# Sliding attention, 32 clips: heads taken in alternating order, the value products one clip later, and the output's bias copy on ACT between the exponentials

## What is computed

```
h  = token block(x)                 # top-k attention, feed-forward 512, convolution of 3, max over pairs: 32 x 125 x 128
n  = (h - mean) / sqrt(var + eps)   # over the features
q, k, v = n @ W_qkv + b_qkv
p  = softmax over the keys at most 32 steps away of (q . k) / 4
h  = h + (p @ v) @ W_proj + b_proj
out = h + (h - mean) / sqrt(var + eps)
```

## Time and profile before

| | |
|---|---|
| median of three runs | 547.76 us |
| the profiled execution, its own time | 550.68 us |
| its span, first to last instruction | 548.9 us |
| mean granted TensorE clock, share of full | 0.947 |
| PE / DVE / ACT / POOL busy, whole span | 92% / 74% / 65% / 60% |
| first scores of the sliding attention | 389.45 us |
| last instruction on POOL (output of clip 31) starts | 545.74 us |

### The profile page before, as it was taken

One profiled execution on the slowest core, in us unless ns is written; L12 is line 12 of the kernel. 1 busy time (PEld: TensorE's weight loads), 2 busy tenths in 40 slices (PEclk: granted clock), 3 DMA queues, 4 the chain that ended last, 5 costly groups with the idle time before them and its releaser, 6 DMA issues.

```text
span 548.9 us, 13987 instructions
## 1 busy us (share of the span) xinstructions
PE 503.3 (92%) x4554; PEld 355.3 (65%) x4554; DVE 408.9 (74%) x1728; ACT 358.4 (65%) x1072; POOL 329.2 (60%) x367
## 2 busy tenths in 40 slices
PE   6998899999998599999999999997599999999983
PEld 4778666666665357766667776655367766776762
DVE  3797757888886367787877777865369988898993
ACT  5985558889887244454455445453578888888881
POOL 2860647778886556776666676663126555565654
PEclk9999559999999699999999999999779999999997
DMA  4440212222222010000000000000000000000000
GB/s 163 138 161 11 64 34 51 56 62 62 63 60 75 20 37 20 19 20 22 35 22 20 19 20 20 1 1 1 0 2 2 20 21 20 13 11 21 20 21 20
DMA packets 21946, 19.89 MB, mean 36 GB/s; under 512 B 14210, under 2 KB 18466, under 8 KB 21746
## 3 DMA queue, kind: packets, MB, share of 16 engines
q1 hardware_dynamic: 21298, 18.28, 11.6%
q10 hardware_dynamic: 576, 0.71, 0.4%
HBM read 16.81 MB, written 2.18 MB: 35 GB/s over the span
## 4 chain that ended last, share of the span: by engine, by line
PE 44%; DVE 15%; issue 4%; ACT 2%; POOL 2%; POOLq 0%; DVEq 0%; ACTq 0%
PE quad L802 10%; PE quad L779 9%; PE bank L824 6%; PE bank L888 4%; PE bank L899 4%; DVE quad L1156 4%; PE bank L905 3%; PE quad L771 2%; PE bank L880 2%; DVE z_all L1186 2%; DVE otok L1168 2%; DVE st_all L1188 2%; DVE wmax L1156 2%; PE bank L793 1%; PE bank L817 1%
## 5 line engine op out<-in xcount | busy, mean ns | idle before, releaser
L476 POOL TENSOR_SCALAR put<-keyb,c 100x1000 f32<-100x1000 bf16 x32 | 89.0, 2782 | 47.9 <-DMA keyb<-key_scratch 26.3
L972 ACT ACTIVATE wprobs<-quad,wmax 125x125 f32<-125x125 f32 x256 | 75.5, 372 | 19.7 <-DVE wmax L1156 19.7
L1156 DVE CUSTOM_DVE_ANT_0 quad<-quad,c 125x125 f32<-125x125 f32 x256 | 66.1, 311 | 9.1 <-PE quad L847 9.1
L609 ACT ACTIVATE probs<-quad,negmax 100x250 f32<-100x250 f32 x128 | 58.3, 467 | 21.8 <-DVE negmax L561 20.9
L779 PE MATMUL quad<-h1T,w 128*128 128x500 f32 x128 | 61.9, 609 | 0.7 <-ACT hid L943 0.6
L802 PE MATMUL quad<-w,hid 128*125 128x128 f32 x512 | 58.8, 273 | 0.1
L802 PEld LDWEIGHTS quad<-w,hid 128*125 128x125 f32 x512 | 57.3, 188 | 0.8 <-issue 0.5
L1058 POOL TENSOR_TENSOR kbd<-wkT,c 128x250 f32<-128x250 f32 x32 | 19.2, 600 | 53.0 <-ACT wkT L980 53.0
L491 PE MATMUL bank<-c,probs 100*125 100x100 f32 x256 | 48.3, 316 | 2.2 <-ACT probs L609 1.4
L491 PEld LDWEIGHTS bank<-c,probs 100*125 100x125 f32 x256 | 36.8, 209 | 20.6 <-issue 13.2
L943 ACT ACTIVATE hid<-quad,vec_cols 128x500 f32<-128x500 f32 x64 | 43.0, 675 | 7.4 <-PE quad L779 4.1
(11 more groups left out here) (131 smaller groups left out, 1267.9 us busy)
## 6 DMA issues: line engine op xcount, KB each, us to landing
keyb<-key_scratch SPq DMA_DIRECT2D x64, 97.7 KB
xa<-xT SPq DMA_DIRECT2D x8, 500.0 KB, 3.6
xt<-xtok SPq DMA_DIRECT2D x16, 250.0 KB
out<-o_all SPq DMA_DIRECT2D x7, 250.0 KB
w<-weights SPq DMA_DIRECT2D x1, 1024.0 KB, 7.2
vec_rows<-rows SPq DMA_DIRECT2D x1, 448.0 KB, 5.2
c<-consts ACTq DMA_DIRECT2D x1, 428.5 KB, 6.5
w<-weights ACTq DMA_DIRECT2D x1, 192.0 KB, 4.2
```

What stands on the lines that cost most here:

```text
L476: nc.gpsimd.tensor_scalar(put[u % 3][:, :, :], keyb[p][:, :, :], c[0:ROWS, CONST["sidx"]], None, ALU.is_equal).then_inc(put_done, 1)
L609: nc.scalar.activation(probs[p][:, ch, :], s_bank[ch][0:ROWS, 0:L], ACT.Exp, bias=negmax[p][:, ch:ch + 1], accum_out=rowsum[p][:, ch:ch + ...
L972: ins = nc.scalar.activation(probs[p][:, j, :], s_of(j), ACT.Exp, bias=negmax[p][:, j:j + 1], scale=-1.0)
L1156: ins = nc.vector.tensor_tensor_reduce(s_of(j), s_of(j), c[0:LH, CONST["band"]], 1.0, OFF, ALU.add, ALU.min, negmax[p][:, j:j + 1])
```

## The change

- The order of the heads is a table, ORDER = (0, 2, 4, 6, 1, 3, 5, 7), so that two successive heads lie in different PSUM banks. Each mask and each exponential has its own semaphore count and its own wait; masks 4 to 7 of the order wait for the exponential 0 to 3 that reads the same bank.
- The value products of a clip are issued one window later (u-2), and in PE's queue between the k/q products and the v product. They no longer wait for oF, but for otok of the clip before and oT. vo has three buffers.
- All that follows them (oT, y_a, otok, oF, projection, z, statistics, output) is one window later too, so there is one more window at the end (u = 34 on PE, ACT and DVE, 35 on POOL, each one more than before).
- PE issues the transposes of oT ahead of the transposes of the probabilities. ACT issues oT between kT and qT.
- oF moves from DVE to ACT, behind the exponential number 5 of the order and ahead of numbers 6 and 7.
- On DVE z stands ahead of the copy probsT, the statistics behind it. otok is written in the heads' own order through a permuted access pattern.
- y_of and y_proj lie in columns 256 and 384 of y_bank.

```diff
-        vo = pair("vo_", [LH, H, CW])
+        vo = [sb(f"vo_{i}", [LH, H, CW]) for i in range(3)]
-        y_a, y_of, y_proj = y_bank[0:LH, 256:512], y_bank[:, 0:LH], y_bank[0:LH, 256:256 + D]
+        y_a, y_of, y_proj = y_bank[0:LH, 256:512], y_bank[:, 256:256 + LH], y_bank[0:LH, 384:384 + D]
+        ORDER = (0, 2, 4, 6, 1, 3, 5, 7)
...
@@ PE
+                if within(u, 3, B + 3):
+                    pe.wait_ge(oT_done, u - 2)
+                    for i in range(2):
+                        ins = nc.tensor.transpose(y_a[:, 128 * i:128 * i + 128], oT[:, LH * i:LH * i + LH], ident)
+                    ins.then_inc(otok_ready, 1)
+
                 if within(u, 1, B + 1):
-                    pe.wait_ge(exp_done, 4 * u)
+                    pe.wait_ge(exp_done, H * u)
...
+                if within(u, 2, B + 2):
+                    wait(pe, otok_done, u - 2)
+                    wait(pe, oT_done, u - 2)
+                    pe.wait_ge(pT0_done, u - 1)
+                    pe.wait_ge(pT1_done, u - 1)
+                    pe.wait_ge(v_done, u - 1)
+                    if u == 2:
+                        pe.wait_ge(n3T_done, NP)
+                    for j in range(H):
+                        ins = nc.tensor.matmul(y_bank[CW * (j % 4):CW * (j % 4) + CW, LH * (j // 4):LH * (j // 4) + LH],
+                                               vo[(u - 2) % 3][:, ORDER[j], :], probsT[p][:, j, :], start=True, stop=True)
+                    ins.then_inc(pv_ready, 1)
+
...
-                if within(u, 1, B + 1):
-                    wait(pe, oF_done, u - 1)
-                    pe.wait_ge(pT0_done, u)
-                    pe.wait_ge(pT1_done, u)
-                    pe.wait_ge(v_done, u)
...
-                if within(u, 2, B + 2):
-                    pe.wait_ge(oF_done, u - 1)
+                if within(u, 3, B + 3):
+                    pe.wait_ge(oF_done, u - 2)
                     nc.tensor.matmul(y_proj, oF[:, :], w[:, WEIGHT["wp"]], start=True, stop=True).then_inc(proj_ready, 1)
...
@@ ACT
+                def exponents(lo, hi):
+
+                    for k in range(lo, hi):
+                        j = ORDER[k]
+                        act.wait_ge(min_done, H * u + k + 1)
+                        nc.scalar.activation(probs[p][:, j, :], s_of(j), ACT.Exp, bias=negmax[p][:, j:j + 1], scale=-1.0).then_inc(exp_done, 1)
...
+                if within(u, 3, B + 3):
+                    act.wait_ge(pv_ready, u - 2)
+                    wait(act, otok_ready, u - 3)
+                    wait(act, z_done, u - 3)
+                    nc.scalar.activation(oT[:, :], y_bank[:, 0:2 * LH], ACT.Copy).then_inc(oT_done, 1)
+                if within(u, -1, B - 1):
                     wait(act, scores, u)
                     nc.scalar.activation(qT[pn][:, :], x_q, ACT.Identity, bias=col("wq_b")).then_inc(qT_done, 1)
...
                 if within(u, 0, B):
                     wait(act, pT0_ready, u - 1)
-                    exponents(0)
-                    exponents(1)
+                    exponents(0, 2)
                 if within(u, 1, B + 1):
                     act.wait_ge(pT1_ready, u)
                     wait(act, pv_ready, u - 2)
                     nc.scalar.activation(probsT[1 - p][:, 4:8, :].rearrange("p h l -> p (h l)"), t_bank[1][0:LH, 0:4 * LH], ACT.Copy).then_inc(pT1_done, 1)
                 if within(u, 0, B):
-                    exponents(2)
-                    exponents(3)
+                    exponents(2, 6)
+                if within(u, 3, B + 3):
+                    act.wait_ge(oF_ready, u - 2)
+                    wait(act, proj_ready, u - 3)
+                    nc.scalar.activation(oF[:, :], y_of, ACT.Identity, bias=col("wv_b")).then_inc(oF_done, 1)
+                if within(u, 0, B):
+                    exponents(6, 8)
...
@@ DVE
+                b = u - 3
+                def mask_and_min(lo, hi):
+
+                    for k in range(lo, hi):
+                        j = ORDER[k]
+                        if k >= 4:
+                            dve.wait_ge(exp_done, H * u + k - 3)
+                        nc.vector.tensor_tensor_reduce(s_of(j), s_of(j), c[0:LH, CONST["band"]], 1.0, OFF, ALU.add, ALU.min,
+                                                       negmax[p][:, j:j + 1]).then_inc(min_done, 1)
+                if within(u, 0, B):
+                    dve.wait_ge(scores, u + 1)
+                    mask_and_min(0, 2)
+                if within(u, 3, B + 3):
+                    dve.wait_ge(otok_ready, b + 1)
                     nc.vector.reciprocal(rinv[:, :], y_a.rearrange("p (h f) -> p h f", h=H)[:, :, HD]).then_inc(rinv_done, 1)
+                    dve.wait_ge(rinv_done, b + 1)
+                    wait(dve, oF_ready, b)
+                    nc.vector.tensor_tensor(otok[:, :].rearrange("p (k c f) -> p c k f", k=4, c=2),
...
+                if within(u, 0, B):
+                    mask_and_min(2, 6)
+                if within(u, 0, B):
+                    mask_and_min(6, 8)
+                if within(u, 3, B + 3):
+                    dve.wait_ge(proj_ready, b + 1)
...
+                    nc.vector.tensor_tensor(z_all[:, b:b + 1, :], y_proj.unsqueeze(1), z_all[:, b:b + 1, :], ALU.add).then_inc(z_done, 1)
+                if within(u, 0, B):
                     dve.wait_ge(pT0_ready, u + 1)
                     wait(dve, pv_ready, u - 1)
                     nc.vector.tensor_copy(probsT[p][:, 0:4, :].rearrange("p h l -> p (h l)"), t_bank[0][0:LH, 0:4 * LH]).then_inc(pT0_done, 1)
...
+                if within(u, 3, B + 3):
+                    dve.wait_ge(z_done, b + 1)
+                    nc.vector.bn_stats(zst[:, b, :], z_all[:, b, :]).then_inc(stat, 1)
+                    dve.wait_ge(stat, b + 1)
+                    nc.vector.bn_aggr(mvz[:, b, :], zst[:, b, :]).then_inc(mean_done, 1)
```

More of the change, by code:

```diff
@@ L827, in ffn @@
                     ins.then_inc(conv_ready, 1)
-            pe.wait_ge(ones_in, 2)
+            pe.wait_ge(ones_in, 3)
             def window(h, p):
@@ L844, in window @@
                     pe.wait_ge(kbd_done, u + 1)
-                    wait(pe, exp_done, 4 * u)
+                    wait(pe, exp_done, H * u)
                     for cc in range(4):
@@ L966, in window @@
                 _, _, pn = shift(h, p, 1)
-                def exponents(cc):
-                    act.wait_ge(min_done, 4 * u + cc + 1)
-                    for j in range(2 * cc, 2 * cc + 2):
-                        ins = nc.scalar.activation(probs[p][:, j, :], s_of(j), ACT.Exp, bias=negmax[p][:, j:j + 1], scale=-1.0)
-                    ins.then_inc(exp_done, 1)
+                def exponents(lo, hi):
[3 more added lines that the diff above has]
+                        nc.scalar.activation(probs[p][:, j, :], s_of(j), ACT.Exp, bias=negmax[p][:, j:j + 1], scale=-1.0).then_inc(exp_done, 1)
                 if within(u, -1, B - 1):
@@ L984, in window @@
                     act.wait_ge(v_ready, u + 1)
-                    wait(act, pv_ready, u - 1)
-                    nc.scalar.activation(vo[p][:, :, 0:HD], x_v.rearrange("p (h f) -> p h f", h=H), ACT.Copy).then_inc(v_done, 1)
-                if within(u, 2, B + 2):
-                    act.wait_ge(pv_ready, u - 1)
-                    wait(act, otok_ready, u - 2)
-                    wait(act, z_done, u - 2)
-                    nc.scalar.activation(oT[:, :], y_bank[:, 0:2 * LH], ACT.Copy).then_inc(oT_done, 1)
+                    wait(act, pv_ready, u - 2)
+                    nc.scalar.activation(vo[u % 3][:, :, 0:HD], x_v.rearrange("p (h f) -> p h f", h=H), ACT.Copy).then_inc(v_done, 1)
                 if within(u, 0, B):
                     wait(act, pT0_ready, u - 1)
-                    exponents(0)
-                    exponents(1)
+                    exponents(0, 2)
                 if within(u, 1, B + 1):
@@ L1000, in window @@
                 if within(u, 0, B):
-                    exponents(2)
-                    exponents(3)
+                    exponents(2, 6)
[5 more added lines that the diff above has]
+                    exponents(6, 8)
             in_turn(act, ffn, window)
-            at(window, B)
-            at(window, B + 1)
+            for u in range(B, B + 3):
+                at(window, u)
         @block.gpsimd
@@ L1073, in _ @@
             in_turn(pool, ffn, window)
-            for u in range(B, B + 3):
+            for u in range(B, B + 4):
                 at(window, u)
@@ L1142, in ffn @@
                     stats(1, t2, 4, t + 1)
-            for i in range(2):
+            for i in range(3):
                 nc.vector.memset(vo[i][:, :, HD:CW], 1.0).then_inc(ones_in, 1)
@@ L1148, in window @@
                 u, _, _ = shift(h, p, 0)
-                um2, _, _ = shift(h, p, -2)
-                def mask_and_max(cc):
-                    if cc == 0:
-                        dve.wait_ge(scores, u + 1)
-                    for j in range(2 * cc, 2 * cc + 2):
```

(24 more changed lines are left out.)

44 lines of the change are left out of this document (14 added, 30 removed).

## The result

The kernel after takes 557.08 us (median of four runs, 556.37 to 557.75), the kernel before beside it 547.62 (four runs, 546.08 to 548.02): ratio 1.0178 [1.0153, 1.0203]. It is slower by 9.5 us; the forecast was 555.7, slower by 7.9. The profiled execution took 556.59 us, its span is 554.7. The ratios here leave out executions more than 1.5% above the fastest of their kernel.

What follows compares the result with a forecast made beforehand. Bound taken as a DVE, PE, DVE loop of 4.367 us. New period 4.58: 28 x 0.213 = 6.0, minus 1.5 at the head, plus 3.4 at the tail, +7.9 us, so 555.7 us; range 550.5 to 562.5.

Steps and rivals of the forecast that it cites:

- So +3.4: Tail of the sliding attention: one more window after the last scores was to add 3.4 us.
- The clock rival: Sliding attention: PE idles in each window, its clock drops, and each ten windows cost 25 us; chance 0.03.
- The head: First windows of the sliding attention: 0.9 and 0.6 us saved, 1.5 together.
- The 0.6 forecast for the next window: Window 2 has no z yet, so window 3's first mask follows after 3.84 in place of 4.45 us.
- A second path ties with it.: Kernel before: mask, four exponentials, then probability transposes were said to tie with the DVE, PE, DVE loop at the period, 4.37.
- 0.24 saved at the first exponential: ACT's first exponential waits for one mask instead of two and starts 0.43 us after the first mask.
- 0.57 off the path.: PE's queue: value products moved between the k/q and v products, a clip later, were to leave the chain, saving 0.57 us.
- PE alone, at most 4.2: PE's own work per window, from its 9.66 busy of 10 us, was put at no more than 4.2 us.
- the loop of 4.15 through oT: Loop z, oT, its transposes, otok, value products, back to z, with v product and a hop: 4.15 us.
- Faster: Alternating heads shorten mask and exponential pitches; period towards 4.10, total 542.2 us; chance 0.07.
- No change: Pitches shrink half way, or ACT's order matters less: period 4.26 to 4.34, total within 0.2%; chance 0.03.
- slower, more than forecast: z and copy keep whole durations, masks delay exponentials, or otok's write takes longer: period 4.79, total 561.5 us; chance 0.20.

Runs made afterwards that it cites:

- the early oF: Kernel after with oF one exponential earlier in ACT's queue, behind number 4 of the order: period 4.401, 549.76 us in one run.
- the pair waits: Kernel after, with each exponential again waiting for both masks of its pair: period 4.821, 566.42 us in one run.
- The experiment on the last windows: Kernel after with extra PE transposes into an unread bank in the last windows: 555.89 us, ratio 1.0155 to the kernel before, last scores to end 20.9 us.
- the order alone: Kernel before with only the alternating head order and single counts and waits: period 4.124, 539.83 us over six runs, ratio 0.988.
- with pair waits: Kernel before with the alternating head order, each exponential still waiting for the second mask of its pair: period 4.367, 546.49 us in one run.
- the kernel with the copy ahead of z: Kernel after with DVE's copy of the first four heads' transposed probabilities put back ahead of z: period 4.352, 551.0 us, ratio 1.0048 to the kernel before.

## Why the prediction was right, and where not

**The balance of the change.** The periods of the table form a chain of edits from before to after:

| step | period | difference | over 28 periods |
|---|---|---|---|
| before | 4.367 | | |
| single waits in the new order | 4.124 | -0.243 | -6.8 |
| oF on ACT behind exponential 5 | 4.695 | +0.571 | +16.0 |
| value products a clip later, with PE's and ACT's new order | 4.352 | -0.343 | -9.6 |
| z ahead of the copy: after | 4.575 | +0.223 | +6.2 |

Two gains and two losses. The parts aren't independent: the value products' new place gains 0.34 where oF is late, and costs 0.35 where oF is on DVE.

**Right.** The period: 4.58 forecast, 4.575 measured, and slower, as said. The chain went as written, through ACT from the first exponential to oF, then projection, z, copy, statistics. Forecast and measured: first mask to first exponential 0.43 and 0.42, oF to projection 0.42 and 0.44, z to copy 0.21 and 0.21, copy to statistics 0.59 and 0.59. DVE's wait before z was put at about 1 us, it is 0.94. Only ACT's idle times were put too high: about 0.7 before the first exponential and 0.3 before oT, where the trace has 0.42 and 0.21. That oF waits for ACT alone is shown by the early oF (4.401) and the pair waits (4.821). By the figures of the Trainium skill, "ScalarE: Activation LUTs", What ACT_TABLE_LOAD costs, the pitch of the bias copy was an estimated 0.29; the trace has 0.24 (493.23 to 493.47), so the row decides.

**Right by place, mis-sized: the end.** "So +3.4" measured +6.3. I priced the added window of the end by the earlier trace rows, as if the clock of before held in the kernel after. It went to 0.50 from 538 us on, and the last two steps took 5.00 and 4.01. The clock rival was dismissed for the middle, rightly (1.00 there), and never asked for the end. The experiment on the last windows gives 2.8 of the missing 2.9 us back. That the rest is the forecast +3.4 is partly luck: the 3.69 of the earlier trace rows holds some time at the lower clock itself.

**The head** was forecast at -1.5 and measured -1.1, which is near by luck. From scores 1 to scores 2 it is 5.29 in place of 6.12, the 0.9 forecast for the value products. The 0.6 forecast for the next window did not come: 4.65 in place of 4.45, where the scores of window 2 lasted 1.21 us at the lower clock (390 to 400 us: 0.53), against 0.81 in the earlier trace rows. In its place 0.44 came off the first window (8.71 against 9.15), for which the sum had no term; 0.25 of that goes with the single waits, since the order alone has 8.71 too and with pair waits 8.96.

**Wrong: "A second path ties with it."** The path over otok alone was not at 4.37. Its step of 0.34, from the transpose of otok to the transposes of the probabilities, held 0.18 of waiting for the fourth exponential, and what held the kernel before was the path through ACT. I had noticed that both paths reach the instruction at 494.79 and took this for a tie; an instruction that waits for two inputs has one that is last, and the sum over the other includes the wait. So I wrote down 0.24 saved at the first exponential only as a term of the new chain and did not see that alone it is worth 6.8 us. The forecast was not hurt, as the new chain passes through that step; the reading of the kernel before was.

**Half wrong: "0.57 off the path."** In the kernel after the value products are indeed off the path. But they left one place in the loop between otok and z for another. ACT's queue hides that. With oF on DVE it comes out, as 4.472 shows. The same holds for "PE alone, at most 4.2" and the loop of 4.15 through oT: once z's place is mended, PE's queue with its waits takes 4.352, where the prediction's shorter loops had nothing above 4.2. The loop through oT left out that its z stands behind the copy and the copy behind the transposes of the probabilities.

**The rivals.** *Faster*, by back-to-back heads of one bank being what stretches a mask: no. The pitches are unchanged, and with the order alone but waits in pairs the period is that of before. The Trainium skill, "Perfetto Trace Analysis", Optimizing Scalar/DVE Operations, says that some offload from a saturated DVE to ScalarE may make sense; here the move alone cost 0.57 per period, since DVE, busy 9.07 of 10 us, was not the bound. *No change* and *slower, more than forecast* did not come; z and the copy kept the short pitches.

**The total.** 11.0 us in the sliding attention of the profiled executions, 7.9 forecast; of the 3.1 between them 2.9 are the end. The medians differ by 9.5, so the forecast missed the median by 1.4 only. That it missed by less than 3.1 is luck: the stages ahead, which the change does not touch, scatter by more than that.

## What to carry to other kernels

A step that looks like hardware time between two instructions may be the wait for a third: where two paths meet in one instruction, ask which input came last, and price the other path without the wait. Any closed chain of starts sums to the period, also one with waits in it, so a sum that fits proves nothing; it is the idle time and what ended it, or an experiment, that tells the path. In the kernel before the sum fitted and the path was another. When work is moved between engines, count what stands ahead of it in the new queue, not its duration: oF costs the same on ACT and on DVE, and its place cost 0.57 us per window. A change of several parts can hide one that pays; here the finer waits, in the alternating order, take 1.2% off by themselves, while the whole is 1.8% slower.

## What was not expected of the hardware

**The clock in an end that waits.** In the kernel after PE was busy 7.52 of 10 us between 530 and 540 us at a granted clock of 0.87, and 5.23 of the next 10 at 0.50; before had 1.00 with 7.46 between 530 and 540. Ahead of the fall PE was busy 1.19 of 2 us in after (534 to 536); in before 1.06, 1.22 and 0.84 in the stretches of 2 us from 536 to 542, in the last of which it fell. At the lower level a projection of 0.48 us takes 0.79, as this row of the kernel after, timeline of PE, shows:

```profile
544.34 0.79 PE L908 MATMUL bank<-w,oF 128*125 128x128 f32 x2 [0.46 <-ACT oF L1008]
```

**The unchanged stages scatter by 5 us.** The first scores came at 389.45 in the profiled execution of before and at 384.21 in that of after, and between 384.2 and 389.3 in the experiments. In both traces the clock falls at about 57 us, in the first attention. In before it is still at 0.50 at 80 us and back at 1.00 by 85; in after it is back by 75. Busy time by stretch from 75 to 80 us, first before, then after:

```profile
75.00:80.00 5.00, 5.00 (x57) 3.63 (x56) 2.78 (x8) 3.17 (x11) 2.78 (x1) 0.50 0.14 40
```

```profile
75.00:80.00 5.00, 5.00 (x86) 3.34 (x74) 4.01 (x11) 4.65 (x19) 4.38 (x2) 1.00 0.18 47
```

The longer stretch at the lower level and the later first scores go together by and large: the kernel with the copy ahead of z has both too (0.50 up to 80 us, first scores at 389.3), and in the other experiments the clock of 75 to 80 us is 0.94 or more and the scores come between 384.2 and 387.6. What decides its length was not tried. It means that a single execution's total says little here below 5 us, and that the spacing of windows says much.
